# A four-block graph network on one core: x loaded in half tiles on two queues, one basis unit moved behind an output projection, and a later load of a root weight

## The chip, the cores and the metric

The kernel runs on one core of one Trainium2 chip. The metric is the device time of one execution in microseconds (us), the median of three runs. The core has five engines that work side by side and wait for each other through semaphores: TensorE (PE, matmuls; its weight loads are PEld), VectorE (DVE), ScalarE (ACT), GpSimd (POOL) and SyncE (SP, which only issues transfers). Transfers are issued by SP, ACT or POOL and carried by the core's 16 DMA engines.

## The reference, cut to what matters

Four blocks in a row, each of the form x = x + block(relu(layernorm(x))), on 512 nodes with 512 features and 16,896 edges.

```python
h = relu(layernorm(x)); x = x + attention_block(h)   # L0: masked softmax over axis 1, Wo, LN, FF, LN
h = relu(layernorm(x)); x = x + gin_block(h)         # L1: lin, 2 x (segment_sum, W1, W2, batch norm)
h = relu(layernorm(x)); x = x + gcn(h)               # L2: degree-normed aggregation and a weight
h = relu(layernorm(x)); x = x + rgcn(h)              # L3: two gated relational layers

w = einsum('rb,bio->rio', att, basis)                # L3: 30 bases of 512x512, two relations, two layers
msg_r = sigmoid(x_j @ gate_w[r]) * x_j @ w[r]
out = segment_sum(msg_by_type) + x @ root + bias

attn_out = attention(q, k, v, adj) @ Wo + bo         # Wo: the four output projections named below
```

The relational weights `w` are independent of x. They need all of `basis`, 2 x 31 MB, the bulk of what the kernel reads.

## The kernel before, in words

Everything is held as 128-partition tiles: a 512x512 matrix is four tiles (C = 4). Each engine has its own written-out program and the order on an engine is the order in the code.

**Basis units.** The sum over bases is cut in 64 units. A unit is 1 MB of `basis`, loaded by SP into one of four ring places (`bring`; four units go elsewhere), and eight rows of matmul in the profile (L1357, four matmuls of 32 output columns each, fp32). SP may load unit n only when PE has used unit n - 4 (L343). PE's `units(n)` puts units between other work. Four units fill one PSUM bank; ACT copies the bank into `stage`, SP writes it to `w_scratch`.

**Start.** SP issues x tiles 0 and 2, ACT issues x tiles 1 and 3 and then the three edge arrays (66 KB each), SP then issues column constants, the alphas, 16 tiny transfers of `att` (30 rows of 4 bytes, L331) and the first units (L336). POOL issues four 1 MB weights (L385), waits for all 16 `att` transfers and spreads them into `attw` with three copies (L388); the first unit on PE needs these copies. DVE takes layer norm statistics of each x tile (L853), ACT normalises (L543), PE transposes, and DVE turns the edges into one-hot factors (L891 to L905, then L836 and L839), which PE multiplies 132 times (L1427) to count edges, with the q, k and v projections between them.

**Attention.** It runs in eight steps (`it` = 0..7). In step `it` PE makes the scores of step it + 1 (`products` L1490, `exclude` L1498), multiplies the probabilities of step it - 1 by v (`attend`, L1513) and runs `STEP_UNITS[it]` units. DVE finds the maximum (L962 to L964), centres (L1038), sums (L1049 to L1053) and scales (L1065). In the last step PE has the output projections (`project(0)` and `project(1)`, L1567) around `attend(6)`; then `attend(7)`, one unit, `project(2)` and `project(3)`.

```python
                    if it == 2 * C - 1:
                        project(0)
                    if it:
                        attend(it - 1)
                    if it == 2 * C - 1:
                        project(1)
                    if it < 2:
                        qkv_tile(2 * C + 2 + it)
                    units(STEP_UNITS[it])
```

**Root weights.** `root1` is the weight of x @ root in the first relational layer. POOL loads it (1 MB, L398) once the semaphore that `LAST_READ` names has reached 4: before, the four tiles of the second block's last convolution (`c2_1_psum`). Right after that convolution PE runs two units, four groups of transposes (L1668, the last of which raises `x4_psum` four times), five units, four filler matmuls (`keep_clock`), the first quarter of the GCN aggregation (L1411), a unit, the rest of the aggregation, a unit and the GCN weight stage (L1371). DVE meanwhile adds, normalises and splits h into two parts (L1208), and splits the GCN weight (L1015). ACT copies root1 after the aggregation (L490).

Of the kernel before, what the change touches and what calls it, by code (L numbers as in the profile page):

```python
# [28 lines left out]
P = 128  # L29
N = 512  # L30
D = 512
C = D // P
# [24 lines left out]
def act_hots(n):  # L57

    return n * 15 // 32


def on_act(n):
    return act_hots(n + 1) > act_hots(n)
# [21 lines left out]
def in_extra(n):  # L85

    return any(n in pair for pair in EXTRAS)


RING_UNITS = [n for n in range(2 * UNITS) if not in_extra(n)]  # L90
STEP_UNITS = (1, 2, 3, 3, 3, 3, 3, 0)
ATTENTION_BATCHES = (EARLY_UNITS + sum(STEP_UNITS)) // BATCH + 1
AGG0_BATCHES = 11

# [15 lines left out]
             "f2b": ("weight_parts", 2 * C), "c1_0": ("ff1_psum", C), "lin": ("ff1_psum", 2 * C),  # L110
             "c2_0": ("ff2_psum", C), "c1_1": ("ff2_psum", C),
             "c2_1": ("weight_parts", 7 * C), "gcn": ("weight_parts", 8 * C),
             "root1": ("c2_1_psum", C), "root2": ("c2_1_psum", C)}

AGG2_BANKS = H1T_BANKS = (0, 1, 4, 5)
T_ORDER = ("h1T", "ff1", "ff1_second", "hT2", "agg0", "agg1", "agg2")
# [12 lines left out]
def build(nc, x, src, dst, etype, weights, rows, cols, alphas, att, basis, scratch, out):  # L129
    with ExitStack() as ctx:  # L130
        def sb(name, shape, dt=F32):
            return ctx.enter_context(nc.sbuf_tensor(name, shape, dt))
# [3 lines left out]
        def sem(name):  # L136
            if name not in names:
                names[name] = ctx.enter_context(nc.semaphore(name))
            return names[name]
# [14 lines left out]
        xr = sb("xr", [P, C, D])  # L154
# [161 lines left out]
        with nc.Block() as block:  # L316

            @block.sync
            def _(sp):

                for c in (0, 2):
                    sp.dma_start(xr[:, c, :], x[:, c, :]).then_inc(sem(f"x{c}_loaded"), 16)
                sp.dma_start(colsb[:, :], cols).then_inc(sem("cols_loaded"), 16)
                sp.dma_start(alph[:, :], alphas.partition_broadcast(P)).then_inc(sem("cols_loaded"), 16)
                sp.wait_ge(sem("att_ready"), 1)
# [136 lines left out]
            def _(act):  # L462
# [68 lines left out]


                my_chunks = [n for n in range(ECH) if on_act(n)]
                for c in (1, 3):
                    act.dma_start(xr[:, c, :], x[:, c, :]).then_inc(sem(f"x{c}_loaded"), 16)
                for i, e in enumerate((src, dst, etype)):
                    act.dma_start(edge_i[:, i, :], e).then_inc(sem("edges_loaded"), 16)
                act.wait_ge(sem("small"), 1)
                act.activation(root_of_eps[:, :], eps[:, :], ACT.Sqrt)

# [27 lines left out]
                for n in range(ECH):  # L568
                    if on_act(n):
                        i = act_hots(n)  # L570
# [55 lines left out]
                for it in range(2 * C):  # L626
# [5 lines left out]
                    if it + 1 < 2 * C:  # L632
                        exps(it + 1)
                    stage_units(STEP_UNITS[it])
                    if C - 1 <= it < 2 * C - 1:
# [180 lines left out]
            def _(dve):  # L816
# [58 lines left out]
                    dve.tensor_tensor(vr[:, c, :], bank[v_bank(c)][:, :], row("bv"), ALU.add).then_inc(sem("v"), 1)  # L875

                for c in range(C):
                    dve.wait_ge(sem(f"x{c}_loaded"), 16)
                    norm_stats(0, xr[:, c, :], c)
                    if c == 1:  # L880
                        nbias(0, 0)
                        nbias(0, 1)
# [445 lines left out]
            def _(pe):  # L1328
# [13 lines left out]
                def units(n):  # L1342


                    for u in (next(unit) for _ in range(n)):
                        b, g = divmod(u, BATCH)
                        if u == 0:
                            pe.wait_ge(sem("att_ready"), BATCH)
                        if g == 0 and b >= 2:
                            pe.wait_ge(sem("stage_ready"), b - 1)  # L1350
                        if g == 0 and b == EARLY_UNITS // BATCH:
                            pe.wait_ge(sem("v"), 1)
                        elif g == 0 and b == EARLY_UNITS // BATCH + 1:
                            pe.wait_ge(sem("v"), C)
                        wait_unit(pe, u)
                        for j in range(COLT):
                            mm = pe.matmul(unit_bank(b)[32 * j:32 * j + 32, :], attw[0:KB, u // UNITS, g, :],  # L1357
                                           unit_place(u)[0:KB, j, :], start=(g == 0), stop=(g == BATCH - 1),
                                           tile_position=(0, 32 * j), skip_group_check=True)
                        mm.then_inc(sem("basis_used"), 1)  # L1360
# [198 lines left out]
                def project(c):  # L1559

                    pe.wait_ge(sem("ao"), 2 if c < 2 else 4)
                    if c == 0:
                        need_weight(pe, "o")
                    if c < 2:
                        pe.wait_ge(sem("centred"), 4 * C - 1)
                    for k in range(C):
                        mm = pe.matmul(bank[C + c][:, :], qT[:, k, blk(P, c)], weight("o")[:, k, :], start=(k == 0),  # L1567
                                       stop=(k == C - 1))
                    mm.then_inc(sem("o_psum"), 1)

                pe.wait_ge(sem("no_edge"), C)
                for it in range(2 * C):
                    if it + 1 < 2 * C:
                        for pair in range(2):
                            products(it + 1, pair)
                            exclude(it + 1, pair, "scores_psum")
                    if it == 2 * C - 1:
                        project(0)
                    if it:
                        attend(it - 1)  # L1580
                    if it == 2 * C - 1:
                        project(1)
                    if it < 2:
                        qkv_tile(2 * C + 2 + it)
                    units(STEP_UNITS[it])
                attend(2 * C - 1)
                units(1)
                project(2)
# [218 lines left out]
```

## Time and profile before

| | |
|---|---|
| median of 3 runs | 455.6 us (455.17 to 456.53) |
| profiled execution, its own time | 459.73 us |
| profiled execution, span | 457.9 us |
| PE busy | 441.6 us (96%) |
| DVE busy | 346.4 us (76%) |
| ACT busy | 243.6 us (53%) |
| mean granted TensorE clock | 0.993 of full |
| moved by DMA | 99.22 MB, mean 217 GB/s |

The profile is of one execution; times in it count from the start of its span. A row of a timeline gives start, length, engine, line, operation, tiles, shape, count, and in brackets how long the engine stood idle before it and what released it. Rows of an engine with a "q" are the issue of transfers, not the transfers. Matmul lengths overlap their successors a little, so a group's true cost is the distance to the next start.

### The profile page before, as it was taken

To read this page: it belongs to the slowest core of one execution; us is meant where nothing else is said; L and a number is where in the kernel's file an instruction comes from. 1 tells how busy PE (TensorE), PEld (TensorE's weight loads), DVE (VectorE), ACT (ScalarE), POOL (GpSimd) and SP (SyncE) were. 2 spreads that over 40 slices of the span, in tenths; PEclk is the share of its full clock that TensorE was granted. 3 is DMA by queue.
4 is the path that set the end of the run, shared out by engine and by line. 5 is a ranking of instruction groups with operands and counts; after the bars stand their busy time and mean duration, and the time that the engine had idled before them with its cause. 6 is when DMAs were issued, how large, how long until landed. Compare 5 with 4: busy or idle time off the path is not lost.

```text
span 457.9 us, 6200 instructions
## 1 busy us (share of the span) xinstructions
PE 441.6 (96%) x2226; PEld 275.4 (60%) x2226; DVE 346.4 (76%) x736; ACT 243.6 (53%) x428; POOL 42.7 (9%) x59
## 2 busy tenths in 40 slices
PE   8999999899997999999999999999989999999997
PEld 3334453444432345768756867677357688888885
DVE  5999996899999849785879675766778695866212
ACT  5999994676897516562246335535662523511210
POOL 3240000024224002000010000010000000000000
PEclk9999999999999799999999999999999999999999
DMA  7997348426699747979089856687871740000002
GB/s 258 414 392 170 115 167 324 160 92 233 245 374 353 278 192 250 424 263 383 36 336 342 318 213 285 247 320 284 318 250 49 290 178 16 1 0 2 0 3 92
DMA packets 18090, 99.22 MB, mean 217 GB/s; under 512 B 2959, under 2 KB 3599, under 8 KB 7567
## 3 DMA queue, kind: packets, MB, share of 16 engines
q1 hardware_dynamic: 13191, 72.72, 42.4%
q0 software_dynamic: 4000, 25.18, 14.9%
q10 hardware_dynamic: 864, 0.86, 0.6%
q8 instruction: 22, 0.36, 0.3%
q14 instruction: 13, 0.11, 0.1%
HBM read 93.50 MB, written 5.25 MB: 216 GB/s over the span
## 4 chain that ended last, share of the span: by engine, by line
PE 72%; DVE 14%; DMA 10%; issue 2%; ACT 1%; DVEq 0%; SPq 0%
PE bank L1371 20%; PE sbank L1703 10%; DMA bring<-in_basis 7%; PE bank L1716 6%; PE sbank L1357 6%; PE sbank L1427 6%; PE sbank L1567 4%; PE bank L1688 4%; PE bank L1450 3%; PE bank L1357 3%; PE bank L1411 2%; DVE stat L853 2%; PE sbank L1411 2%; DMA wring<-in_weights 2%; PE bank L1513 2%; PE sbank L1490 2%
## 5 line engine op out<-in xcount | busy, mean ns | idle before, releaser
L1357 PE MATMUL sbank<-bring,attw 120*32 120x512 f32 x336 | 41.0, 599 | 2.2 <-DMA bring<-in_basis 2.2
L839 DVE TENSOR_SCALAR cnt<-iota_row,edge_f 128x512 bf16<-128x512 f16 x132 | 41.2, 347 | 0.4 <-PE sbank L1427 0.4
L466 ACT ACTIVATE stat<-stat,eps 128x1 f32<-128x1 f32 x32 | 9.4, 294 | 42.9 <-DVE stat L858 42.9
L1427 PE MATMUL sbank<-cnt,adjT 128*128 128x512 bf16 x132 | 30.6, 380 | 0.3
L576 ACT ACTIVATE adjT<-distance,edge_w,edge_f 128x128 bf16<-128x128 bf16 x61 | 29.3, 480 | 1.4 <-PE sbank L1427 1.4
L1281 DVE SCALAR_TENSOR_TENSOR y_lo<-sbank,gate,y_hi 128x512 fp32r<-128x512 f32 x16 | 11.8, 750 | 22.6 <-ACT y_hi L765 22.5
L497 ACT ACTIVATE s<-bank,colsb 128x512 f32<-128x512 f32 x24 | 16.4, 687 | 21.8 <-PE bank L1371 21.8
L1427 PEld LDWEIGHTS sbank<-cnt,adjT 128*128 128x128 bf16 x132 | 12.3, 98 | 21.7 <-DVE cnt L839 6.4
L1371 PE MATMUL bank<-hT_hi,w_hi 128*128 128x512 f32 x64 | 25.3, 395 | 0.0
L529 ACT ACTIVATE distance<-iota_row,edge_f 128x128 bf16<-128x128 f16 x61 | 24.3, 400 | 1.8 <-DVE edge_f L905 0.4
L1371 PE MATMUL bank<-hT_hi,w_lo 128*128 128x512 f32 x64 | 24.9, 390 | 0.0
L1371 PE MATMUL bank<-hT_lo,w_hi 128*128 128x512 f32 x64 | 24.9, 389 | 0.0
L1703 PE MATMUL sbank<-w_hi,xT_hi 128*128 128x512 f32 x64 | 24.9, 389 | 0.0
L1703 PE MATMUL sbank<-w_lo,xT_hi 128*128 128x512 f32 x64 | 24.9, 389 | 0.0
L1703 PE MATMUL sbank<-w_hi,xT_lo 128*128 128x512 f32 x64 | 24.9, 389 | 0.0
L836 DVE TENSOR_SCALAR adjT<-iota_row,edge_f,edge_w 128x128 bf16<-128x128 f16 x71 | 22.1, 312 | 2.0 <-PE sbank L1427 2.0
L765 ACT ACTIVATE y_hi<-sbank,gate 128x512 fp32r<-128x512 f32 x16 | 10.8, 688 | 23.8 <-PE sbank L1703 23.8
L1357 PE MATMUL bank<-bring,attw 120*32 120x512 f32 x144 | 19.0, 627 | 4.0 <-DMA bring<-in_basis 4.0
L600 ACT ACTIVATE s<-s 128x1024 f32<-128x1024 f32 x16 | 16.9, 1058 | 11.1 <-DVE s L1038 10.6
L426 POOL TENSOR_TENSOR s<-s,row_sum 128x1024 f32<-128x1024 f32 x7 | 16.6, 2374 | 59.1 <-ACT row_sum L610 59.1
L1357 PEld LDWEIGHTS sbank<-bring,attw 120*32 120x32 f32 x336 | 8.5, 109 | 22.0 <-issue 20.2
L1490 PE MATMUL sbank<-qkw 64*128 64x256 f32 x128 | 18.1, 402 | 2.1 <-DVE s L1038 2.0
(250 smaller groups left out, 1095.9 us busy)
## 6 DMA issues: line engine op xcount, KB each, us to landing
bring<-in_basis SPq DMA_DIRECT2D x59, 1024.0 KB, 9.7
wring<-in_weights POOLq DMA_DIRECT2D x8, 1024.0 KB, 10.0
landing<-in_weights POOLq DMA_DIRECT2D x4, 1024.0 KB, 5.1
w_scratch<-stage SPq DMA_DIRECT2D x16, 256.0 KB
hT<-in_weights POOLq DMA_DIRECT2D x4, 1024.0 KB, 8.4
qkw<-w_scratch POOLq DMA_DIRECT2D x2, 2048.0 KB, 8.0
rring<-in_rows POOLq DMA_DIRECT2D x12, 256.0 KB, 8.3
wring<-in_basis SPq DMA_DIRECT2D x2, 1024.0 KB, 12.9
```

Of the source, the lines that this page charges most:

```text
L529: act.activation(distance[:, i % 2, :], iota[:, 0:P], ACT.Abs, scale=-1.0, bias=dst_lo[:, n:n + 1]).then_inc(sem("distance"), 1)
L576: act.activation(hot_d[:, n % HOT, :], distance[:, i % 2, :], ACT.Relu, scale=minus_w[:, n:n + 1], bias=weight_f[:, n:n + 1]).then_inc(sem ...
L836: dve.tensor_scalar(hot_d[:, n % HOT, :], iota[:, 0:P], dst_lo[:, n:n + 1], weight_f[:, n:n + 1], ALU.is_equal, ALU.mult).then_inc(sem("ho ...
L839: dve.tensor_scalar(hot_s[:, n % HOT, :], iota[:, :], src_f[:, n:n + 1], None, ALU.is_equal).then_inc(sem("hot_ready"), 1)
L1357: mm = pe.matmul(unit_bank(b)[32 * j:32 * j + 32, :], attw[0:KB, u // UNITS, g, :], unit_place(u)[0:KB, j, :], start=(g == 0), stop=(g == ...
L1371: mm = pe.matmul(bank[c][:, :], lhs[:, k, blk(P, c)], rhs[:, k, :], start=(k == 0 and i == j), stop=(k == C - 1 and i == 1))
L1411: mm = pe.matmul(bank[banks[c]][:, :], x[:, k, blk(P, c)].bitcast(dt), counts[:, k, :], start=(k == 0 and i == 0), stop=(k == C - 1 and i ...
L1427: pe.matmul(bank[7][:, :], hot_d[:, n % HOT, :], hot_s[:, n % HOT, :], start=(n == 0), stop=(n == ECH - 1)).then_inc(sem("hot_used"), 1)
L1490: pe.matmul(sbank[:, place_of(h), :], kT[at:at + HD, h // 2, blk(P, m)], qT[at:at + HD, h // 2, blk(NH, half_n)], start=(a == 0), stop=Fal ...
L1567: mm = pe.matmul(bank[C + c][:, :], qT[:, k, blk(P, c)], weight("o")[:, k, :], start=(k == 0), stop=(k == C - 1))
L1703: mm = pe.matmul(bank[C + c][:, :], (xT_hi, xT_lo)[i][:, k, blk(P, c)], (w_hi, w_lo)[j][:, rel * C + k, :], start=(k == 0 and i == j), sto ...
L1716: mm = pe.matmul(bank[c][:, :], counts[:, k, blk(P, c)], y[:, k, :].bitcast(dt), start=False, stop=(rel == RELS - 1 and k == C - 1 and i = ...
```

## The change

Four edits. (1) Each x tile is loaded as two halves of 64 partitions, the upper by SP and the lower by ACT, tiles in order 0 to 3 on both; DVE waits for both halves. (2) The three edge loads go from ACT's queue to SP's, behind the x halves and ahead of the constants, `att` and the units. (3) `STEP_UNITS` takes one unit from step 5 and gives one to step 7, and in step 7 that unit stands between `project(0)` and `attend(6)`; ACT's staging follows the same table. (4) `root1` is loaded on `x4_psum` instead of `c2_1_psum`.

```diff
-STEP_UNITS = (1, 2, 3, 3, 3, 3, 3, 0)
+STEP_UNITS = (1, 2, 3, 3, 3, 2, 3, 1)
...
-             "root1": ("c2_1_psum", C), "root2": ("c2_1_psum", C)}
+             "root1": ("x4_psum", C), "root2": ("c2_1_psum", C)}
...
-                for c in (0, 2):
-                    sp.dma_start(xr[:, c, :], x[:, c, :]).then_inc(sem(f"x{c}_loaded"), 16)
+                for c in range(C):
+                    sp.dma_start(xr[0:P // 2, c, :], x[0:P // 2, c, :]).then_inc(sem(f"x{c}_loaded"), 16)
+                for i, e in enumerate((src, dst, etype)):
+                    sp.dma_start(edge_i[:, i, :], e).then_inc(sem("edges_loaded"), 16)
...
-                for c in (1, 3):
-                    act.dma_start(xr[:, c, :], x[:, c, :]).then_inc(sem(f"x{c}_loaded"), 16)
-                for i, e in enumerate((src, dst, etype)):
-                    act.dma_start(edge_i[:, i, :], e).then_inc(sem("edges_loaded"), 16)
+                for c in range(C):
+                    act.dma_start(xr[P // 2:P, c, :], x[P // 2:P, c, :]).then_inc(sem(f"x{c}_loaded"), 16)
...
-                    dve.wait_ge(sem(f"x{c}_loaded"), 16)
+                    dve.wait_ge(sem(f"x{c}_loaded"), 32)
...
                     if it == 2 * C - 1:
                         project(0)
+                        units(STEP_UNITS[it])
                     if it:
                         attend(it - 1)
...
-                    units(STEP_UNITS[it])
+                    if it < 2 * C - 1:
+                        units(STEP_UNITS[it])
```

How it moves the order, at three places. First TensorE in step 5 of the attention (L1513 is `attend`, L1357 units, L1490 and L1498 the next scores), the difference:

```order
 L1498 MATMUL sbank<-no_edge,never 128x512 x2
 L1513 MATMUL bank<-s,vr 64x256 x8
-L1357 MATMUL bank<-bring,attw 32x512 x12
+L1357 MATMUL bank<-bring,attw 32x512 x8
 L1490 MATMUL sbank<-qkw 128x256 x4
 L1498 MATMUL sbank<-no_edge,never 128x512 x2
```

Step 5 has two units instead of three. Then TensorE in step 7, the difference (L1567 is a projection, the first row is the units of step 6):

```order
 L1357 MATMUL bank<-bring,attw 32x512 x12
 L1567 MATMUL sbank<-wring,qkw 128x512 x4
+L1357 MATMUL bank<-bring,attw 32x512 x4
 L1513 MATMUL bank<-s,vr 64x256 x8
 L1567 MATMUL sbank<-wring,qkw 128x512 x4
```

The units of step 6 are now 22, 23 and 24 (before 23, 24 and 25), and unit 25 stands behind the first projection. Last, SP's queue from its start, before:

```order
L318 UNCONDITIONAL_BRANCH
L322 DMA xr<-in_x 128x512 x2
L323 DMA colsb<-in_cols 128x64
L324 DMA alph<-in_alphas 128x2
L331 DMA attw<-in_att 30x1 x16
L336 DMA bring<-in_basis 128x2048 x12
```

and now:

```order
L322 DMA xr<-in_x 64x512 x4
L324 DMA edge_i<-in_src 128x132
L324 DMA edge_i<-in_dst 128x132
L324 DMA edge_i<-in_etype 128x132
L325 DMA colsb<-in_cols 128x64
L326 DMA alph<-in_alphas 128x2
L333 DMA attw<-in_att 30x1 x16
```

Five more transfers stand ahead of `att` and the units on SP's queue.

## Rows read from the trace of the kernel before

**Rows 1.** The page: busy time by engine; TensorE, its clock and GB/s in 40 slices.

```profile
PE 441.6 (96%) x2226; PEld 275.4 (60%) x2226; DVE 346.4 (76%) x736; ACT 243.6 (53%) x428; POOL 42.7 (9%) x59
...
PE   8999999899997999999999999999989999999997
...
PEclk9999999999999799999999999999999999999999
...
GB/s 258 414 392 170 115 167 324 160 92 233 245 374 353 278 192 250 424 263 383 36 336 342 318 213 285 247 320 284 318 250 49 290 178 16 1 0 2 0 3 92
```

**Rows 2.** Timeline of TensorE, steps 5 to 7 of the attention.

```profile
138.80 1.06 PE L1357 MATMUL bank<-bring,attw 120*32 120x512 f32 x8 [1.50 <-DMA bring<-in_basis]
...
144.88 1.07 PE L1357 MATMUL bank<-bring,attw 120*32 120x512 f32 x8
146.98 1.06 PE L1357 MATMUL bank<-bring,attw 120*32 120x512 f32 x8 [1.03 <-DMA bring<-in_basis]
149.36 1.94 PE L1357 MATMUL bank<-bring,attw 120*32 120x512 f32 x8 [1.31 <-DMA bring<-in_basis]
151.22 5.97 PE L1567 MATMUL sbank<-wring,qkw 128*128 128x512 f32 x8
157.12 1.95 PE L1513 MATMUL bank<-s,vr 128*64 128x256 f32 x16
159.00 3.70 PE L1567 MATMUL sbank<-wring,qkw 128*128 128x512 f32 x8
```

**Rows 3.** Timeline of VectorE, steps 6 and 7: centring, last scaling.

```profile
137.34 2.35 DVE L1038 TENSOR_TENSOR s<-sbank,softmax_tmp 128x1024 f32<-128x1024 f32 x2
...
145.65 2.36 DVE L1038 TENSOR_TENSOR s<-sbank,softmax_tmp 128x1024 f32<-128x1024 f32 x2
...
154.15 2.28 DVE L1065 TENSOR_TENSOR s<-s,row_sum 128x2048 f32<-128x2048 f32 x1
```

**Rows 4.** Windows: us, PE, PEld, DVE, ACT, POOL busy, PEclk, DMA share, GB/s.

```profile
148.00:150.00 2.00, 0.69 (x7) 0.20 (x8) 2.00 (x3) 1.96 (x3) 0.43 (x1) 0.75 0.97 389
150.00:152.00 2.00, 2.00 (x9) 0.50 (x2) 1.93 (x4) 1.51 (x3) 0.00 (x0) 0.50 0.91 324
```

**Rows 5.** Timeline of the end of the second block and the GCN aggregation.

```profile
321.06 0.53 POOL L398 DMA_DIRECT2D wring<-in_weights  x1 [18.93 <-PE bank L1371]
...
329.49 1.07 PE L1357 MATMUL sbank<-bring,attw 120*32 120x512 f32 x8 [0.90 <-DMA bring<-in_basis]
...
334.63 1.06 PE L1357 MATMUL sbank<-bring,attw 120*32 120x512 f32 x8 [1.29 <-DMA bring<-in_basis]
...
338.02 2.49 DVE L1015 TENSOR_TENSOR w_lo<-landing,w_hi 128x512 fp32r<-128x512 f32 x4
...
340.67 1.29 DVE L1028 TENSOR_TENSOR hT_lo<-bank,hT_hi 128x512 fp32r<-128x512 f32 x2 [0.16 <-ACT hT_hi L497]
...
341.96 2.20 ACT L490 CAST root_hi<-wring 128x512 fp32r<-128x512 f32 x4
```

**Rows 6.** Timeline of the start, all engines.

```profile
0.74 0.86 SPq L322 DMA_DIRECT2D xr<-in_x  x2
...
2.73 7.73 SPq L331 DMA_DIRECT2D attw<-in_att  x16
...
4.62 0.69 DVE L853 BATCH_NORM_STATS2 stat<-xr 128x6 f32<-128x512 f32 x1 [4.62 <-DMA xr<-in_x]
...
10.59 0.22 DVE L891 CAST edge_f<-edge_i 128x132 f32<-128x132 int32 x1
...
19.86 1.56 POOL L388 COPY attw<-attw 120x16 f32<-120x16 f32 x3 [14.60 <-DMA attw<-in_att]
...
23.53 1.06 PE L1357 MATMUL sbank<-bring,attw 120*32 120x512 f32 x8
```

**Rows 7.** DMA issues: queue, count, KB each, median us to landing.

```profile
attw<-in_att SPq DMA_DIRECT2D x16, 0.1 KB, 8.0
...
edge_i<-in_etype ACTq DMA_DIRECT2D x1, 66.0 KB, 5.8
```

## The prediction

> **What bounds the kernel now.** I read the page first: TensorE is busy 96% of the span and no other engine more than 76% [rows 1], so a change pays only where it takes idle or slowed time off TensorE. The line of the clock shows one slice of 40 below full, the fourteenth (slices of 11.4 us, so 149 to 160) [rows 1]. So I looked for TensorE's waits for basis units, and for the time at half clock. The chain of work that ended last runs over `bring` loads at two of the places that the change touches, and these two stretches and the start are all that matters.
>
> In steps 5 to 7 of the attention TensorE waits 1.50 us for unit 22, 1.03 for unit 24 and 1.31 for unit 25 [rows 2]. Unit 25 lands at 149.36; until then nothing behind it can run, although project(0) has all it needs once VectorE's second-last centring half is done: the two halves of the last centring start at 145.65 and take 2.36 together, so the bank is free from about 146.9 [rows 3]. In the same place the granted clock falls from full to 0.50 (0.75 as a mean over 148 to 150, so at about 149) [rows 4], after TensorE was busy 0.69 of 2.00 us: that is 1.2 instead of 2.4 GHz. Unit 25 takes 1.94 instead of 1.06 and project(0) until 157.12 instead of the 3.63 that project(1) takes at full clock [rows 2].
>
> **The unit behind the projection.** Unit 22 moves from step 5 to step 6 and unit 25 behind project(0); the count of units stays. In step 5 TensorE ends at 137.3 and not at 139.8, which wins nothing: the next scores need the centring that starts at 137.34 [rows 3], so they begin at about 138.5, and VectorE, which works without a pause here (2.00 of 2.00 us [rows 4]), sets when the step ends. Step 6 then runs attend(5), units 22 and 23 (both landed by 144.88 [rows 2], since 23 ran then without a wait) until about 145.7, and waits for unit 24, which lands at 146.98. Its load is triggered by the use of unit 20, which does not move. So unit 24 runs from 146.98 to 148.0 as before, and now project(0) follows at once, 148.0 to 151.6; unit 25 has been there since 149.36 and costs 1.0 behind it. The 1.31 of waiting is covered. Attend(6) (1.9) and project(1) (3.6) follow; attend(7) starts at 158.2. It needs the last scaling, done at 156.43 [rows 3], so there is 1.7 us of slack before VectorE becomes the bound. Bounds for this term: nothing (if unit 24 lands later by what unit 25 waited), or 1.31 and up to 0.9 more, if unit 24 lands sooner because unit 26, now asked for only at 144.7 instead of 139.9, doesn't run beside it. I take 1.35, near the wait that a row shows. Everything behind (f1b's weight on attend(7), f2a's on project(3)) is triggered by TensorE and moves with it.
>
> **The clock** is a term of its own. At full clock unit 25 would have cost 0.9 less and project(0) 2.27 to 2.5 less: 3.2 to 3.4 in this execution. The change leaves one gap of 1.3 us before unit 24 in place of two in 3.4 us, and elsewhere TensorE had gaps of 1.50 (before 138.80) and 1.29 (before 334.63) without losing the clock [rows 2, 5]. So I expect that it doesn't fall here now. But I doubt that the timed runs pay this at all: the profiled execution took 459.73, the three timed ones 455.17 to 456.53, and the difference to the median, 4.1, is about those 3.4. Three runs within 1.4 us hardly hold a mix of both. If the runs never had the slow stretch, its removal brings them nothing. I take 0 here and make the full 3.4 the first rival. "TensorE: Matmul & The Clock Gate" of the Trainium skill (Part 1) says that the moment of the switch varies from run to run of one kernel, which no single trace can show; by it alone an average over runs would hold part of the 3.4.
>
> **The later root weight.** root1 goes out at 321.06, ahead of units 59 and 60, for which TensorE then waits 0.90 and 1.29 [rows 5]. It is first read at 341.96 [rows 5], so it is 15 us early or more. Now it waits for the last transposes, which end at about 325, so unit 59 (asked for at 321.8) has the engines to itself, and unit 60 shares them with root1 for part of its way; 1 MB is 2.5 us at the 414 GB/s of a full slice [rows 1]. Both waits should go, 2.2 us. Not all reaches the end. With no wait the aggregation's last quarter needs VectorE's fourth split at 338.0, and then comes VectorE's split of the GCN weight, 338.02 for 2.49, and behind it the lower parts of the aggregation (340.67) [rows 5], which start at 340.5 at best and let the GCN stage start at 341.2 instead of 342.35. So 1.15 of 2.2 is worth anything; below, nothing, if unit 60 lands no sooner. I take 1.15, since unit 60 has to land only 1.1 us sooner for it. root1 lands by about 333 and its reader is at 341 or later. Nothing else waits behind it: POOL's next wait is for the GCN stage.
>
> **The start.** The first statistics wait for x tile 0 until 4.62 [rows 6]. With halves 256 KB instead of 512 KB are under way first, at the 258 GB/s of the first slice [rows 1] about 0.9 us sooner. TensorE has filler until 7.3 and gains 0.3 there, VectorE 0.7. Against it stands SP's queue: two more x issues (0.43 each) and three edge issues (0.48 each, as an `att` issue) ahead of `att`, so all of the 16 `att` issues, which now begin at 2.73 and take 7.73 [rows 6], begin at 5.0. The last landed when POOL started its copies, 19.86; 2.3 later is 22.1, the copies (1.56) end at 23.7, and TensorE wanted its first unit at 23.53 [rows 6]. So what was gained is lost at that wait: 0.15 slower. The edges, issued 0.7 later, land at about 3.4 + 5.8 = 9.2 [rows 7], VectorE wants them at 9.9 (10.59 less 0.7 [rows 6]). Bounds: 0.7 faster, if `att` is not later; 4.5 slower, if small transfers in one queue behind each other add their landing times instead of sharing, as in the second rival. "DMA: Bandwidth & Descriptors" of the Trainium skill (Issuing engines are not separate DMA queues) says that spreading transfers over issuers only saves issue time; by that, moving the edges costs the 1.45 us of issue and nothing in the transfers. The same page (Queues, rings and completion order) says that each DMA engine takes turns between the queues with work, and by that the small transfers lose the turns that ACT's queue had: the rule behind the second rival.
>
> **Sum** against the profiled execution: 1.35 + 1.15 - 0.15 = 2.35 faster, and 3.4 more for the clock there, so its own time would go from 459.7 to about 454. The timed median stands 4.1 below the profiled time; I take 2.35 off it: 455.6 - 2.35 = 453.2. This case's own range is 452.2 to 454.6.
>
> **Rivals.** (a) The timed runs pay the slow clock before and not after: 455.6 - 2.35 - 3.4 = 449.8. For it: the trace shows it, and it hangs on gaps that every run has. Against: the profiled time stands above the timed ones by its size. (b) SP's queue becomes the bound at the start. Place: the edges, ahead of which four x halves now stand, then constants and 16 `att` transfers, all in one queue beside POOL's 4 MB of weights. Each us by which the edges land behind 10.6, or the last `att` behind 22.0, goes one to one to the end, since TensorE is at 9 tenths or more in every slice from 23 to 80 [rows 1]. From 3.9 us on it makes the whole slower (2.5 are won elsewhere, 1.4 is the bound of no change); at the upper bound of 4.5 the time is 455.6 + 4.5 - 2.5 = 457.6. For it: an `att` transfer of 0.1 KB took 8.0 us to land, an edge array of 66 KB only 5.8 [rows 7], and the last `att`, issued by 10.46, landed 9.4 later [rows 6]. Against: landing is paced by issue too, and the edges' slack was 2 us. (c) The waits only move: unit 24 or 60 lands as much later as the order frees, or VectorE holds the end; then 455.0. For it: the DMA engines are at 0.91 to 0.97 of their time [rows 4] and the bytes are the same.
>
> **Chances.** Forecast 0.46, (a) 0.34, (c) 0.13, (b) 0.07. A measurement of this kernel can tell about 0.3%, 1.4 us, from no change, so faster is below 454.2. The forecast is there in 0.85 of its cases, (a) always, (c) in a few: 0.75 faster. Same 0.18, slower 0.07. The range reaches from a little under (a), 449.3, to the upper end of (c), 455.5.
>
> **What would show it.** Right: in the changed trace no idle time before the unit behind project(0); project(0) starting at about 148 and taking 3.6; attend(7) at about 158; waits before units 59 and 60 below 0.3; the GCN stage 1.1 us sooner relative to the transposes; POOL's copies of `attw` at about 22. Wrong: TensorE idle before its first unit by over 1 us or the edges releasing VectorE (b); the wait before unit 24 grown to 2 us or more (c); a time near 450 (a).

## The result and the profile after

| | before | after |
|---|---|---|
| median | 456.06 us (4 runs, 455.17 to 456.70) | 467.27 us (4 runs, 466.60 to 467.76) |
| profiled execution, its own time | 459.73 us | 466.60 us |
| profiled execution, span | 457.9 us | 464.8 us |
| mean granted TensorE clock in it | 0.993 | 0.992 |

The ratio after to before is 1.0246, with an interval of 1.0226 to 1.0266. The change costs 11.2 us. The time lies outside the predicted range and on the other side of no change. Here and in the table of the experiments the ratios leave out the five executions that ran far slower at a low clock (494 to 734 us), the medians don't.

The page of after, against [rows 1]: span, busy time by engine, TensorE and its clock in 40 slices of 11.6 us.

```profile
span 464.8 us, 6204 instructions
...
PE 443.2 (95%) x2226; PEld 277.0 (60%) x2226; DVE 346.3 (74%) x736; ACT 243.5 (52%) x428; POOL 40.6 (9%) x59
...
PE   7789999989998989999999999999979999999997
...
PEclk9899999999999999999999999999989999999999
```

The busy times are the old ones within 2.1 us. What is new is idle time of TensorE in the first three slices, in two of which VectorE too lost ground, and a clock below full in the second and the thirtieth slice instead of the fourteenth.

The timeline of the start, all engines, against [rows 6]:

```profile
0.74 2.78 SPq L322 DMA_DIRECT2D xr<-in_x  x4
0.74 2.50 ACTq L537 DMA_DIRECT2D xr<-in_x  x4
...
3.01 2.25 POOL L387 DMA_DIRECT2D wring<-in_weights  x4 [0.24 <-issue]
...
4.64 0.69 DVE L853 BATCH_NORM_STATS2 stat<-xr 128x6 f32<-128x512 f32 x1 [4.64 <-DMA xr<-in_x]
4.66 0.61 SPq L324 DMA_DIRECT2D edge_i<-in_etype  x1
...
10.94 0.69 DVE L853 BATCH_NORM_STATS2 stat<-xr 128x6 f32<-128x512 f32 x1 [2.78 <-DMA xr<-in_x]
...
19.10 0.23 DVE L891 CAST edge_f<-edge_i 128x132 f32<-128x132 int32 x1 [5.28 <-DMA edge_i<-in_etype]
...
28.59 3.60 PE L1450 MATMUL bank<-hT,wring 128*128 128x512 f32 x8
```

Issuing four half tiles takes 2.50 to 2.78 us on each queue, where two whole ones took 0.86 on SP's and 0.89 on ScalarE's. So the first of the three edge loads goes out at 3.56, after POOL has begun to issue its 4 MB of weights at 3.01. The first statistics start at 4.64 and not earlier than before (4.62), and those of the last x tile wait 2.78 us. VectorE gets its edges at 19.10 instead of 10.59, and stands idle 5.28 us for them after it had nothing else left. The last row is TensorE's second group of projection matmuls, at 28.59; before, it stood at 20.00. So the start costs 8.6 us. The slow clock of the second slice (from 13 to 17, after 3.06 us in which TensorE stood idle) costs nothing more here, since the edges weren't there yet. The chain of work that ended last in after has one transfer at the start:

```profile
4.66 14.41 DMA edge_i<-in_etype
```

The DMA issues of after (queue, count, KB each, median us to landing) have the same in one number, against 5.8 in [rows 7]:

```profile
attw<-in_att SPq DMA_DIRECT2D x16, 0.1 KB, 9.5
...
edge_i<-in_src SPq DMA_DIRECT2D x1, 66.0 KB, 10.1
edge_i<-in_dst SPq DMA_DIRECT2D x1, 66.0 KB, 12.1
edge_i<-in_etype SPq DMA_DIRECT2D x1, 66.0 KB, 14.4
```

The timeline of TensorE in after around the last attention step, against [rows 2]:

```profile
154.89 1.07 PE L1357 MATMUL bank<-bring,attw 120*32 120x512 f32 x8 [0.89 <-DMA bring<-in_basis]
155.89 3.70 PE L1567 MATMUL sbank<-wring,qkw 128*128 128x512 f32 x8
159.52 1.07 PE L1357 MATMUL bank<-bring,attw 120*32 120x512 f32 x8
160.51 1.95 PE L1513 MATMUL bank<-s,vr 128*64 128x256 f32 x16
162.39 3.70 PE L1567 MATMUL sbank<-wring,qkw 128*128 128x512 f32 x8
166.02 1.95 PE L1513 MATMUL bank<-s,vr 128*64 128x256 f32 x16
...
170.68 7.13 PE L1567 MATMUL sbank<-wring,qkw 128*128 128x512 f32 x16 [1.71 <-ACT qkw L621]
```

Unit 25 stands behind project(0) without a wait and the clock stays at full. But project(2) waits 1.71 us for ScalarE's copy of the attention output (`take_ao`, L621). It starts at 170.68 against 165.75 before: 4.9 us late, so 3.7 of the 8.6 came back here. By the prediction's estimate 3.2 to 3.4 of these are the slow stretch that the profiled execution of before had.

The timeline of TensorE in after at the GCN aggregation, and POOL's load of root1 between, against [rows 5]:

```profile
325.13 1.92 PE L1357 MATMUL sbank<-bring,attw 120*32 120x512 f32 x16
...
332.84 1.04 PE L1357 MATMUL sbank<-bring,attw 120*32 120x512 f32 x8
...
339.85 1.06 PE L1357 MATMUL sbank<-bring,attw 120*32 120x512 f32 x8 [2.97 <-DMA bring<-in_basis]
...
341.53 0.63 PE L1411 MATMUL bank<-adjT_r,root_hi 128*128 128x512 f32 x1
...
349.13 0.50 PE L1371 MATMUL bank<-w_hi,hT_hi 128*128 128x512 f32 x1
```

```profile
329.75 0.53 POOL L400 DMA_DIRECT2D wring<-in_weights  x1 [23.18 <-PE bank L1670]
```

Unit 59 (332.84) no longer waits. Unit 60 (339.85) waits 2.97 instead of 1.29, and behind this longer gap the clock fell, as windows of after show (us, then PE, PEld, DVE, ACT, POOL busy, PEclk, DMA share, GB/s):

```profile
342.00:344.00 2.00, 2.00 (x6) 1.60 (x5) 2.00 (x4) 0.29 (x1) 0.00 (x0) 0.50 0.94 213
```

From the first unit behind the convolution (325.13) to the GCN weight stage (349.13) it takes 24.00 us; before it took 21.59 (320.70 to 342.29). I call this the **GCN distance** below. In this one pair of executions the parts are 8.6 at the start, 3.7 back in the attention, 0.5 more back (most of it at one wait for a weight, which took 10.00 us to land before, issued at 202.33, and 9.55 in after, issued at 207.22), and 2.4 at the GCN: 6.8, of 6.87 measured. The medians differ by 11.2, since the profiled execution of before stands 3.7 above its median and that of after 0.7 below.

### The profile page after: what moved, and what is told of

Its sections match the earlier page's. It is cut to its first block, busy times and chain, and to the rows that moved or that the text cites. A ratio compares the mean times of both kernels' runs of the same rounds, so it can differ in the third digit from the quotient of the medians.

```text
span 464.8 us, 6204 instructions
## 1 busy us (share of the span) xinstructions
PE 443.2 (95%) x2226; PEld 277.0 (60%) x2226; DVE 346.3 (74%) x736; ACT 243.5 (52%) x428; POOL 40.6 (9%) x59
## 4 chain that ended last, share of the span: by engine, by line
PE 64%; DVE 22%; DMA 8%; issue 3%; ACT 1%; SPq 1%; DVEq 0%
PE bank L1371 20%; PE sbank L1705 9%; PE bank L1718 6%; PE sbank L1357 6%; PE sbank L1427 6%; PE bank L1690 4%; DMA edge_i<-in_etype 3%; DVE s L1038 3%; PE bank L1450 3%; DMA bring<-in_basis 3%; PE bank L1411 2%; PE sbank L1411 2%; DMA wring<-in_weights 2%; DVE softmax_tmp L962 2%; DVE stat L853 2%
## 5 line engine op out<-in xcount | busy, mean ns | idle before, releaser
L1357 PE MATMUL sbank<-bring,attw 120*32 120x512 f32 x336 | 41.0, 599 | 3.0 <-DMA bring<-in_basis 3.0
L1427 PE MATMUL sbank<-cnt,adjT 128*128 128x512 bf16 x132 | 32.1, 381 | 2.7 <-DVE cnt L839 1.8
L1281 DVE SCALAR_TENSOR_TENSOR y_lo<-sbank,gate,y_hi 128x512 fp32r<-128x512 f32 x16 | 11.8, 750 | 22.6 <-ACT y_hi L765 22.5
L600 ACT ACTIVATE s<-s 128x1024 f32<-128x1024 f32 x16 | 16.9, 1058 | 11.4 <-DVE s L1038 10.9
L1357 PEld LDWEIGHTS sbank<-bring,attw 120*32 120x32 f32 x336 | 8.6, 109 | 22.5 <-issue 22.5
L1490 PE MATMUL sbank<-qkw 64*128 64x256 f32 x128 | 18.2, 402 | 3.8 <-DVE s L1038 3.8
L1490 PEld LDWEIGHTS sbank<-qkw 64*128 64x128 f32 x128 | 11.1, 186 | 14.4 <-DVE s L1038 8.0
```

The source lines that it names most:

```text
L1427: pe.matmul(bank[7][:, :], hot_d[:, n % HOT, :], hot_s[:, n % HOT, :], start=(n == 0), stop=(n == ECH - 1)).then_inc(sem("hot_used"), 1)
L1490: pe.matmul(sbank[:, place_of(h), :], kT[at:at + HD, h // 2, blk(P, m)], qT[at:at + HD, h // 2, blk(NH, half_n)], start=(a == 0), stop=Fal ...
```

## The experiments

Each kernel is the one before with the edit shown, run in turn with the one before on the same chip (e9 and e10 on another chip than e1 to e8). Runs counts those of the kernel; before has 29 beside e1 to e4, 28 beside e5 to e8, 21 beside e9 and e10.

| kernel | runs | median us | before beside it | ratio, interval |
|---|---|---|---|---|
| e1_start_only | 4 | 464.89 | 456.26 | 1.0192, 1.0146 to 1.0238 |
| e2_unit_only | 12 | 456.51 | 456.26 | 1.0006, 0.9985 to 1.0027 |
| e3_root_only | 12 | 459.16 | 456.26 | 1.0063, 1.0044 to 1.0083 |
| e4_whole_edges_sp | 10 | 456.26 | 456.26 | 0.9994, 0.9968 to 1.0021 |
| e5_halves_edges_act | 4 | 465.82 | 456.55 | 1.0214, 1.0161 to 1.0267 |
| e6_start_hold | 11 | 459.00 | 456.55 | 1.0048, 1.0027 to 1.0069 |
| e7_unit_ao | 12 | 454.60 | 456.55 | 0.9953, 0.9934 to 0.9972 |
| e8_root_after60 | 11 | 460.29 | 456.55 | 1.0074, 1.0040 to 1.0107 |
| e9_unit_ao_rootsp | 10 | 452.80 | 455.98 | 0.9939, 0.9919 to 0.9958 |
| e10_ao_only | 12 | 456.00 | 455.98 | 1.0003, 0.9985 to 1.0021 |

### e1_start_only: edits 1 and 2 alone

```diff
-                for c in (0, 2):
-                    sp.dma_start(xr[:, c, :], x[:, c, :])...
+                for c in range(C):
+                    sp.dma_start(xr[0:P // 2, c, :], x[0:P // 2, c, :])...
+                for i, e in enumerate((src, dst, etype)):
+                    sp.dma_start(edge_i[:, i, :], e)...
...
-                for c in (1, 3):
-                    act.dma_start(xr[:, c, :], x[:, c, :])...
-                for i, e in enumerate((src, dst, etype)):
-                    act.dma_start(edge_i[:, i, :], e)...
+                for c in range(C):
+                    act.dma_start(xr[P // 2:P, c, :], x[P // 2:P, c, :])...
```

> Only the start of the change (x in halves on two queues, the three edge loads on SP's queue); units and root1 as before. Theory S (the start is nearly the whole loss): the changed kernel's edge arrays landed at 19.1 us and VectorE began its one-hots at 20.65 where it had begun at 12.14, so this kernel is 8 to 9 us slower than before, 464 to 465.5, with the same landing of the edges. Rival R (the start is only a part, and the three edits add up differently, as the 11.2 us of the timed runs against the 8.5 suggests): 4 to 6 us slower here, the rest with the other two edits.

It costs 8.6 us, by its interval (from 4 runs) 6.7 to 10.9: the start alone is about three quarters of the result. Its timeline of VectorE shows the same wait:

```profile
18.07 0.23 DVE L891 CAST edge_f<-edge_i 128x132 f32<-128x132 int32 x1 [5.29 <-DMA edge_i<-in_etype]
```

### e2_unit_only: edit 3 alone

```diff
-STEP_UNITS = (1, 2, 3, 3, 3, 3, 3, 0)
+STEP_UNITS = (1, 2, 3, 3, 3, 2, 3, 1)
...
                         project(0)
+                        units(STEP_UNITS[it])
...
-                    units(STEP_UNITS[it])
+                    if it < 2 * C - 1:
+                        units(STEP_UNITS[it])
```

> Only the unit moved behind project(0); start and root1 as before. Forecast of the prediction: 1.35 us faster in the timed runs (454.7), project(0) at about 148 at full clock, attend(7) at 158. Rival V (VectorE is the bound of the attention's end, so that the wait taken away was worth less than 1 us): within 0.7 us of before. Rival N: the gap merely moves before unit 24 and grows to over 2 us: slower.

No measurable difference. TensorE's timeline of it has what the prediction wanted, and then the wait that eats it:

```profile
147.53 3.70 PE L1567 MATMUL sbank<-wring,qkw 128*128 128x512 f32 x8
...
157.66 1.95 PE L1513 MATMUL bank<-s,vr 128*64 128x256 f32 x16
...
162.46 7.13 PE L1567 MATMUL sbank<-wring,qkw 128*128 128x512 f32 x16 [1.86 <-ACT qkw L621]
```

ScalarE's timeline of it says why:

```profile
157.96 0.29 ACT L466 ACTIVATE stat<-stat,eps 128x1 f32<-128x1 f32 x1 [2.71 <-DVE stat L858]
161.15 0.29 ACT L466 ACTIVATE stat<-stat,eps 128x1 f32<-128x1 f32 x1 [2.90 <-DVE stat L858]
161.35 1.05 ACT L621 COPY qkw<-bank 128x512 f32<-128x512 f32 x2
```

attend(7) is over by about 159.6, but the two copies of its result stand on ScalarE behind a square root (L466) that waits for VectorE's statistics of the second projected tile until 161.15. VectorE works without a pause from 149.4 to 162.8, so its statistics aren't sooner, the copies aren't, and neither is project(2). Rival V named VectorE, and it is VectorE that the copies waited for, but only through the order on ScalarE, as the next run shows.

### e7_unit_ao: edit 3, and ScalarE's order mended

The same, and one line moved on ScalarE, so that the copies stand ahead of that square root:

```diff
                 root(1, 0)
-                root(1, 1)
                 take_ao(1)
+                root(1, 1)
                 root(1, 2)
```

> The moved unit alone, and ACT copies the attention's second half for project(2) (take_ao, L621) before the square root of tile 1 instead of behind it. In the run with the moved unit alone TensorE stood 1.86 us before project(2), since ACT waited for VectorE's statistics of tile 1 (161.15) with the copies behind it. Theory A (that order on ACT ate what the moved unit won): the wait falls to 1.1 us or less, project(2) starts 1.5 us sooner, and the kernel is 1 to 1.7 us faster than before. Rival V (VectorE's norm chain holds the end anyway): within 0.4 us of before.

2.0 us faster; by its interval 1.3 to 3.0. Some 0.3 of it can be the clock: all 11 runs in its ratio have 0.999 or more, of before 16 of 27, and those have a median of 456.3. The copies now wait for attend(7) alone, and project(2) starts at 161.11, which is 1.35 sooner than in e2_unit_only, where 1.5 was expected (ScalarE's, then TensorE's timeline of it):

```profile
159.99 1.07 ACT L621 COPY qkw<-bank 128x512 f32<-128x512 f32 x2 [1.77 <-PE bank L1513]
```

```profile
161.11 7.13 PE L1567 MATMUL sbank<-wring,qkw 128*128 128x512 f32 x16 [0.18 <-ACT qkw L621]
```

### e10_ao_only: ScalarE's order alone

The diff is the one of e7_unit_ao, without edit 3.

> Only ACT's copies for project(2) ahead of the square root of tile 1; units where they were. Theory A (the unit and the order on ACT hide each other, so each alone is worth little): within 0.6 us of before, since TensorE still waits for unit 25 before project(0) and attend(7) ends when ACT's square root is free anyway. Rival: the order on ACT alone was worth the whole 1.7 to 2 us and the moved unit nothing: 1.5 us or more faster than before.

Nothing again: here unit 25 holds TensorE, and the copies are in time for it. In its timeline of TensorE:

```profile
149.13 1.06 PE L1357 MATMUL bank<-bring,attw 120*32 120x512 f32 x8 [1.29 <-DMA bring<-in_basis]
...
162.38 7.13 PE L1567 MATMUL sbank<-wring,qkw 128*128 128x512 f32 x16 [0.18 <-ACT qkw L621]
```

The start of project(2) is 162.46 with the unit moved, 162.38 with the copies moved, 161.11 with both. With neither, at full clock, it is 162.72 in e3_root_only and 162.65 in e4_whole_edges_sp. Each of the two waits hid the other.

### e3_root_only: edit 4 alone

```diff
-             "root1": ("c2_1_psum", C), "root2": ("c2_1_psum", C)}
+             "root1": ("x4_psum", C), "root2": ("c2_1_psum", C)}
```

> Only root1 loaded on x4_psum. The prediction said 1.15 us faster. Theory C, from the changed kernel's trace (unit 60 asked for at 327.2 landed at 339.7 together with root1, TensorE idle 2.97 before it, clock at 0.50 after): 1.5 to 3 us slower than before, with the wait before unit 60 at 2.5 to 3.5 us. Rival P (that wait was an accident of the shifted start): 0 to 1.2 us faster.

2.9 us slower. TensorE's and POOL's timelines of it:

```profile
332.41 1.07 PE L1357 MATMUL sbank<-bring,attw 120*32 120x512 f32 x8 [2.67 <-DMA bring<-in_basis]
```

```profile
322.62 0.54 POOL L398 DMA_DIRECT2D wring<-in_weights  x1 [23.18 <-PE bank L1668]
```

Unit 60 was issued at 320.04 and root1 at 322.62, while unit 60 was still under way; unit 60 landed at 332.3, 12.2 after its issue (before 11.75, with root1 issued 1.7 ahead of it). The GCN distance is 22.10, 0.5 more than before. The profiled execution (457.58, its fastest) has a mean clock of 1.000. The other 11 of 12 show a mean clock of 0.996 or less and a median of 459.2; of before 10 of 28 runs did. So 1.6 of the 2.9 goes with the lower clock, as far as one run at full clock can tell. Of the other 1.3 the trace shows 0.5 as waiting, and 0.8 stays open (runs of before at full clock spread by more). The profile of after has a slow stretch right behind unit 60's wait; of e3's own slow runs there is no trace, so that this is their place is argued from after, not shown.

### e8_root_after60: root1 asked for only when unit 60 has been used

```diff
-             "root1": ("c2_1_psum", C), "root2": ("c2_1_psum", C)}
+             "root1": ("basis_used", 61), "root2": ("c2_1_psum", C)}
```

> root1 loaded once unit 60 has been used, so that it shares the DMA engines with neither unit 59 nor unit 60. Theory B (unit 60 is late because root1 takes turns with it): unit 60 lands within 10 us of its issue instead of 11.7 to 12.5, TensorE's wait before it is below 1.5 us, and the kernel is 0.5 to 1.5 us faster than before unless root1 itself lands too late. Rival O (unit 60 is late because of its own queue: unit 59, the stage write and the units issued behind it): it lands 11 us or more after its issue whatever root1 does, TensorE waits over 2 us, and the kernel is no faster than before.

The half of the expectation on unit 60 holds: it lands 9.8 after its issue and its wait is 0.27. The GCN distance falls to 20.56, 1.03 less than before. But root1 is now too late, issued at 332.24 and landed 13.0 later. The rows of unit 60 on TensorE and of root1 on ScalarE:

```profile
330.85 1.06 PE L1357 MATMUL sbank<-bring,attw 120*32 120x512 f32 x8 [0.27 <-DMA bring<-in_basis]
```

```profile
345.30 2.19 ACT L490 CAST root_hi<-wring 128x512 fp32r<-128x512 f32 x4 [6.16 <-DMA wring<-in_weights]
```

What ScalarE does for the relational block stands behind that row, and TensorE waits 2.83 us for ScalarE before 353.37. Behind this wait the clock falls, as windows of this kernel show; its profiled execution also had the slow stretch at project(0) that before had, and all 10 runs in its ratio have a mean clock below 0.999.

```profile
354.00:356.00 2.00, 2.00 (x13) 0.60 (x16) 1.93 (x6) 1.04 (x3) 0.00 (x0) 0.50 0.93 393
```

It is 3.7 us slower in all.

### e4_whole_edges_sp: edges on SP's queue, x tiles whole

```diff
                 for c in (0, 2):
                     sp.dma_start(xr[:, c, :], x[:, c, :])...
+                for i, e in enumerate((src, dst, etype)):
+                    sp.dma_start(edge_i[:, i, :], e)...
...
-                for i, e in enumerate((src, dst, etype)):
-                    act.dma_start(edge_i[:, i, :], e)...
```

> x in whole tiles as before, but the three edge loads behind SP's two x tiles instead of ACT's. They are issued between 1.6 and 3.1 us, before or just as POOL's weights go out (3.0). Theory W (edges are late because they are issued after the 4 MB of weights and must take turns with them): they land at 8 to 10 us and the kernel is within 1.5 us of before. Rival Q (edges are late because they share SP's queue with the many small transfers behind them): they land after 13 us and the kernel is 3 us or more slower.

No difference: standing on SP's queue isn't by itself what delays the edges. They go out at 1.65 to 2.77, ahead of POOL's weights, and land in 4.4 us, at 6.2 to 7.2, sooner than Theory W had them (the DMA issues of this kernel; the second row is the constants, issued behind them):

```profile
edge_i<-in_etype SPq DMA_DIRECT2D x1, 66.0 KB, 4.4
...
colsb<-in_cols SPq DMA_DIRECT2D x1, 32.0 KB, 5.7
```

### e5_halves_edges_act: half tiles, edges left on ScalarE's queue

```diff
-                for c in (0, 2):
-                    sp.dma_start(xr[:, c, :], x[:, c, :])...
+                for c in range(C):
+                    sp.dma_start(xr[0:P // 2, c, :], x[0:P // 2, c, :])...
...
-                for c in (1, 3):
-                    act.dma_start(xr[:, c, :], x[:, c, :])...
+                for c in range(C):
+                    act.dma_start(xr[P // 2:P, c, :], x[P // 2:P, c, :])...
```

> x in halves on two queues, the three edge loads left on ACT's queue, behind its four halves, so they are issued at about 3.3 to 4.8 us as in the changed kernel, after POOL's weights (3.0), but with no small transfers behind them in their queue. Theory W (late issue behind the start of the weights is what delays the edges): they land after 12 us and the kernel is 3 us or more slower than before. Rival Q (sharing SP's queue is what delays them): they land by 10 us and the kernel is within 1.5 us of before.

The whole loss, 9.3 us, with SP's queue holding no edge. They stand on ScalarE's queue and go out from 3.56, behind four half tiles (the DMA issues again):

```profile
edge_i<-in_etype ACTq DMA_DIRECT2D x1, 66.0 KB, 14.8
...
colsb<-in_cols SPq DMA_DIRECT2D x1, 32.0 KB, 10.0
```

The constants allow a finer comparison. They are on SP's queue in both kernels and go out at the same moment, just behind the start of POOL's weights (3.01), but behind two whole tiles and the edges in e4_whole_edges_sp and behind four half tiles in e5_halves_edges_act. SP's timelines, e4 and then e5:

```profile
3.24 0.43 SPq L325 DMA_DIRECT2D colsb<-in_cols  x1
```

```profile
3.28 0.59 SPq L323 DMA_DIRECT2D colsb<-in_cols  x1
```

They land in 5.7 us behind the whole tiles and in 10.0 behind the halves. So the moment of issue isn't the whole cause: the half tiles have a part in it, most likely as unfinished work ahead in the same queue. The slowest of the half tiles takes 7.0 to 8.1 us to land (e1_start_only, after, e5), the slowest whole tile of e4 5.4, and the slowest half with the weights held 4.7 (e6_start_hold). No run issues the edges late behind whole tiles, so how the loss divides between the late issue and the halves ahead isn't shown.

### e6_start_hold: edits 1 and 2, and POOL's weights held until the edges are there

```diff
+                pool.wait_ge(sem("edges_loaded"), 48)
                 for i in range(4):
```

> The start of the change alone, but POOL issues its four weights only when the edge arrays have landed. Theory W: without the weights beside them the edges land at 7 to 9 us on the very queue on which they took until 18.1; the weights then land some 5 us later than before, the q projection starts at 15 to 17 us, and the kernel is 2 to 5 us slower than before instead of 8.7. Rival Q (the queue itself): the edges land after 12 us still, the weights later still, and the kernel is over 10 us slower than before.

The edges go out exactly as in e1_start_only, at 3.57 to 4.67, and land in 3.5 to 4.0 us instead of 9.0 to 13.2, with POOL's weights not yet issued:

```profile
edge_i<-in_etype SPq DMA_DIRECT2D x1, 66.0 KB, 3.5
```

VectorE takes them at 10.68, as before, and about 6 of the 8.6 us are back (the medians stand 2.4 and 8.6 above those of before beside them). What is left is the price of the hold itself: the weights go out at 8.47 instead of 3.01, and TensorE's first projection waits 2.13 us for the first of them and then runs partly at 0.50 of the clock. Windows of this kernel:

```profile
14.00:16.00 2.00, 2.00 (x4) 0.80 (x5) 2.00 (x11) 1.94 (x6) 0.00 (x0) 0.66 1.00 398
16.00:18.00 2.00, 2.00 (x4) 0.91 (x3) 2.00 (x8) 1.94 (x6) 0.00 (x0) 0.50 0.89 307
```

### e9_unit_ao_rootsp: e7_unit_ao, and root1 on SP's queue right behind unit 60

```diff
                         load_unit(n, f"basis{r % BATCH}_loaded")
+                    if n == 60:
+                        sp.wait_ge(sem("c2_1_psum"), C)
+                        sp.dma_start(weight("root1"), weights[WEIGHTS.index("root1")]).then_inc(
+                            sem("root1_loaded"), 16)
...
-                load_weight("root1")
```

> The moved unit, ACT's copies first, and root1 loaded by SP right behind unit 60 on the same queue, instead of by POOL on a queue of its own. Theory B (root1 on another queue takes turns with unit 60 and costs it 2.4 us; nothing else was wrong with loading it later): unit 60 lands about 10 us after its issue, TensorE waits under 0.5 us before units 59 and 60, root1 lands before ACT wants it (no wait on it), the GCN stage starts 1.1 us sooner relative to the second block's end, and the kernel is 0.8 to 1.4 us faster than the one without this edit (454.6), about 453.5, and 2.5 to 3.3 us faster than before. Rival T (the bytes are the bound wherever they stand): units 61 to 63 or root1 are late in its place, and the time is 454.6 or more.

452.8 us, 3.2 faster than before and 14.5 under the change's median. TensorE's timeline of it, units 59 and 60, and SP's:

```profile
321.56 1.04 PE L1362 MATMUL sbank<-bring,attw 120*32 120x512 f32 x8
...
325.79 1.07 PE L1362 MATMUL sbank<-bring,attw 120*32 120x512 f32 x8 [0.19 <-DMA bring<-in_basis]
```

```profile
316.43 0.61 SPq L349 DMA_DIRECT2D wring<-in_weights  x1
```

Root1 is issued 0.5 us behind unit 60, 2.1 sooner after it than in e3_root_only, and yet unit 60 lands in about 9.7 us (e7_unit_ao, with root1 ahead of it on POOL's queue: 11.5): behind it in the same queue, root1 doesn't take from it. The GCN distance is 20.56, in e7_unit_ao it was 21.40. ScalarE reads root1 without a wait. All 10 runs have a clock of 0.999 or more. Against e7_unit_ao the medians say 1.2 us more gain, but their intervals overlap and they were run in different sets and on different chips; that root1's part adds to the gain is shown by the trace and not by the timed ratios.

## Why the prediction was wrong, step by step

**The start: wrong, and it decides.** Predicted 0.15 slower with bounds of 0.7 faster and 4.5 slower; measured 8.6 slower alone. The step that failed is "the edges, issued 0.7 later, land at about 3.4 + 5.8 = 9.2". Two terms of it were false. The issue: I took 0.43 per half tile from whole tiles, and the rows show 2.50 to 2.78 for four, 0.63 to 0.70 each, so the last edge load goes out at 4.66 and not at 3.4. By itself that was harmless: 4.66 + 5.8 = 10.5, just before VectorE took the edges in before. But the 5.8 belonged to loads issued while POOL's weights had not started or had just. The landing time isn't a property of the load but of what is under way beside it: 3.5 to 4.0 (weights held), 4.4 (issued before them, behind whole tiles), 9.0 to 14.8 (issued behind their start, behind four halves). The upper bound of 4.5 took a queue that adds landing times; e5 shows that the loss comes without an edge on SP's queue, and e6 that it goes when the weights are held. Late issue and the half tiles ahead in the queue came together in every run that lost, and the constants of e4 and e5 show that the halves have a part in it. Rival (b) had the place, and the rate of one to one: the edges landed 8.5 behind 10.6 and the start took 8.6. It named the four halves ahead of the edges and POOL's weights beside them, which e6 and the constants bear out. It was wrong on SP's small transfers, which e5 does without, and on the size, which it had at half. Had I placed the issues against POOL's row, 3.01, the risk would have been in plain sight. `att` was late too (POOL's copies at 24.1, forecast 22.1), but the edges were later still.

The rule of the Trainium skill that I cited ("DMA: Bandwidth & Descriptors", Issuing engines are not separate DMA queues) is borne out by e4, where moving the edges cost nothing (ratio 0.9994). The rule of the same page of the Trainium skill that each DMA engine takes turns between the queues with work (Queues, rings and completion order) fits e6 against e1 (3.5 to 4.0 us against 9.0 to 13.2), and e9 against e3 (9.7 against 12.2); I used it only for the small transfers that leave ScalarE's queue, and the sum has no term for POOL's.

The gain that the halves were for is hardly there either: the first statistics start at 4.64, in e1 at 4.39, against 4.62; and the later tiles come later (10.94 for the last, 7.83 before; with the weights held, in e6, it is 7.9).

**The unit behind the projection: mechanism right, sum wrong.** Forecast: project(0) at 148.0, attend(7) at 158.2, no wait for unit 25. Without the late start (e2) they stand at 147.53 and 157.66. The 1.35 was to be followed by everything behind, and this is the step that failed: project(2) has another input, and ScalarE's queue, in which the copy stands behind a wait for VectorE, had no slack. I had named VectorE's slack for attend(7) and not ScalarE's for project(2). With that wait out of the way the gain is 2.0 (e7; 1.7 against the runs of before at full clock), so the size was nearly right.

**The clock: right for the stretch that the change removes.** I took 0 for the timed runs. e2 has no slow stretch in its profile, and no gain. Runs of before show a mean clock of 0.999 or more in 52 of 76, with a median of 456.1 in the first set; the 459.73 with 0.993 was an unlucky one. Rival (a) is out for this reason. What the sum had no term for is the clock that the change itself loses: all four runs of after have a mean clock of 0.988 to 0.992, all four of e1 0.989 to 0.996.

**The later root weight: wrong sign.** Forecast 1.15 faster, measured 2.9 slower alone (e3). "Unit 60 has to land only 1.1 us sooner" failed: counted from the first unit behind the convolution it ran 0.5 later. I let root1 share the engines "for part of its way" and priced nothing for unit 60. Root1 issued 2.6 us behind it on another queue makes it land 12.2 after its issue (e3). With root1 out of the way it takes 9.8 (e8), and in before, with root1 ahead of it, it took 11.75. So the edit kept the collision that it was to lessen, and the gain on unit 59 ended at the next wait. The 1.15 itself was good: where unit 60 isn't disturbed, the GCN stage comes 1.03 sooner (e8, e9). And the longer wait goes with a lower clock in most runs, for which the sum had no term here: that gaps of 1.50 and 1.29 kept the clock says nothing of one of 2.7 to 3.0.

**Rival (c)**, with 0.13, had the mechanism of both later edits, that the waits only move: in e2 to a copy behind VectorE's statistics, in e3 to unit 60. Its price for that, 455.0 or nearly no change, held for e2 and not for e3.

**Sum.** The parts alone give 8.6 + 0.25 + 2.9 = 11.8; the change measured 11.2. The interval of e1 alone is 4 us wide, so these show only that nothing large comes from their meeting.

## What to carry to other kernels

A load's landing time in a profile holds for its moment of issue: before moving or splitting a small load, line up its new issue time with the start of the next large transfer on any queue, look at what will stand unfinished ahead of it in its own queue, and count issue time for the split pieces from rows of their own shape. A wait that is removed pays only up to the next input of the next instruction; look at every queue that feeds it, and at what stands ahead in that queue, before adding up. To keep a second transfer from delaying an urgent one, try it behind that one in the same queue (e9); delaying its issue on another queue only moved the collision here (e3), or made it late itself (e8).

## What the runs showed of the hardware

- A 66 KB load (128 rows of 528 bytes), issued behind four half tiles and 0.5 to 1.8 us after 4 MB of weights began on another queue, takes 9.0 to 14.8 us to land; with the weights held (e6) 3.5 to 4.0. One of 1 KB, the alphas, took 13.8 in after.
- At the same moment of issue, beside the same weights, a 32 KB load took 5.7 us behind whole tiles (e4) and 10.0 behind half tiles (e5).
- A load of half the partitions costs more issue time than one of all: 0.63 to 0.70 us a piece against 0.43, so four halves hold a queue's issuer three times as long as two whole tiles, also where the weights are held (e6: 2.50 and 2.78 us).
- A wait of about 2.7 us at unit 60 (e3, full clock in 1 of 12 runs) goes with a lower clock in nearly every run; with waits of 0.90 and 1.29 us there, 24 of 76 runs of before show less than 0.999, and the profiled execution of before lost it elsewhere, in the attention. Behind a wait of 2.83 us e8 runs at 0.50.
